# First edge pass of a graph network: target numbers spread over the partitions by TensorE instead of by a broadcast DMA

## The reference, cut to what matters

```
ef = concat([x[src], x[dst]], axis=1)        # 100000 x 256
h  = ef @ W1.T + b1
h  = relu(batchnorm(h, g1, be1))             # mean and variance over the edges
h  = h @ W2.T + b2
eu = relu(batchnorm(h, g2, be2))
x  = layernorm(x + segment_sum(eu, dst, n))
```

## Time and profile before

| | us |
|---|---|
| median of 3 runs | 4250.56 |
| lowest, highest | 4240.57, 4261.32 |
| span of the profiled execution | 4243.9 |
| first edge pass in it | 977 to 1502 |

### The profile page before, as it was taken

One profiled execution on the slowest core, in us unless ns is written; L12 is line 12 of the kernel. 1 busy time (PEld: TensorE's weight loads), 2 busy tenths in 40 slices (PEclk: granted clock), 3 DMA queues, 4 the chain that ended last, 5 costly groups with the idle time before them and its releaser, 6 DMA issues. The chain is left out here.

```text
span 4243.9 us, 85956 instructions
## 1 busy us (share of the span) xinstructions
PE 3447.9 (81%) x20439; PEld 1689.6 (40%) x20548; DVE 2654.4 (63%) x3759; ACT 1496.2 (35%) x2093; POOL 1050.2 (25%) x1132
## 2 busy tenths in 40 slices
PE   3777767686677978888898998599889989989996
PEld 1333333243344556666645554233322233332223
DVE  6877766522233455554202223699989989989995
ACT  2134555601122222222202111221088851208883
POOL 3877774665555412221000001000010000000000
PEclk8989999978898999999899999799999999999998
DMA  2255665667787866666583774511054331103333
GB/s 62 93 168 196 213 224 193 222 248 255 240 276 253 304 214 200 179 175 171 187 276 130 246 257 143 148 61 54 23 140 132 115 116 54 62 16 128 117 123 73
DMA packets 373635, 688.38 MB, mean 162 GB/s; under 512 B 136131, under 2 KB 223297, under 8 KB 372769
## 3 DMA queue, kind: packets, MB, share of 16 engines
q1 hardware_dynamic: 236400, 361.19, 26.8%
q10 hardware_dynamic: 112052, 274.54, 18.8%
q0 software_dynamic: 25088, 51.43, 4.8%
HBM read 453.91 MB, written 208.37 MB: 156 GB/s over the span
## 5 line engine op out<-in xcount | busy, mean ns | idle before, releaser
L823 POOL DMA_INDIRECT gat<-a_table,gidx x592 | 674.3, 1139 | 259.3 <-issue 142.5
L1703 DVE SCALAR_TENSOR_TENSOR pw<-ex,c_full 128x1564 f32<-128x1564 f32 x400 | 680.8, 1779 | 35.6 <-ACT ex L1231 30.9
L1231 ACT ACTIVATE ex<-psum 128x782 f32<-128x782 f32 x800 | 610.4, 826 | 77.4 <-PE psum L2114 58.9
L1665 DVE CUSTOM_DVE_ANT_0 masked<-psum,masks 128x1784 bf16<-128x1784 f32 x320 | 551.7, 1784 | 64.8 <-ACT masks L1204 43.7
L1752 PE MATMUL psum<-one_src,one_dst 128*128 x1968 | 417.7, 351 | 208.9 <-DVE one_dst L1399 127.6
L1397 DVE TENSOR_SCALAR one_src<-iota_sub,src_low 128x800 f16 x984 | 382.6, 430 | 191.7 <-PE psum L1752 124.7
L2123 PE MATMUL psum<-pw,vaug 128*32 128x391 f32 x3200 | 348.6, 508 | 30.2 <-DVE pw L1703 10.0
L1752 PEld LDWEIGHTS psum<-one_src,one_dst 128*128 x1968 | 189.4, 100 | 422.9 <-issue 340.4
L1539 DVE SCALAR_TENSOR_TENSOR u<-psum,u 128x1024 f16<-128x1024 f32 x98 | 120.0, 1225 | 254.8 <-ACT u L1109 254.8
L1204 ACT ACTIVATE masks<-masks,far 128x3128 bf16<-128x3128 bf16 x40 | 115.5, 2900 | 423.4 <-DMA masks<-ct_parts 423.4
L1067 ACT ACTIVATE r<-psum,vec 128x1024 f32<-128x1024 f32 x98 | 118.0, 1205 | 398.7 <-PE psum L1898 331.4
(11 more groups left out here) (357 smaller groups left out, 4792.0 us busy)
## 6 DMA issues: line engine op xcount, KB each, us to landing
c_full<-c_whole SPq DMA_DIRECT2D x80, 977.5 KB, 5.0
r_edges<-r ACTq DMA_DIRECT2D x98, 512.0 KB
r_in<-r_edges ACTq DMA_DIRECT2D x98, 512.0 KB, 3.7
c_ring<-ct_parts SPq DMA_DIRECT2D x100, 480.0 KB, 4.4
c_whole<-c_sum ACTq DMA_DIRECT2D x100, 400.0 KB
a_edges<-gat SPq DMA_DIRECT2D x148, 256.0 KB, 2.6
a_in<-a_edges ACTq DMA_DIRECT2D x74, 512.0 KB, 5.6
c_ring<-ct_parts SPq DMA_DIRECT2D x100, 320.0 KB, 3.6
```

Of the source, the lines that this page charges most:

```text
L823: g.indirect_dma_start(to, None, a_table, bass.IndirectOffsetOnAxis(ap=gidx[:, s, k:k + 1], axis=0)).then_inc(landed, 16)
L1231: a.activation(ex[:, step_slot(n // 2), (n % 2) * 2 * CW:(n % 2 + 1) * 2 * CW].rearrange("p (h t) -> p h t", h=2), psum[:, o:o + 2 * BANK] ...
L1665: v.tensor_tensor_reduce(out=masked[:, n % 2, 0:count * width].rearrange("p (c t) -> p c t", c=count), in0=psum[:, first * BANK:(first + c ...
L1703: v.scalar_tensor_tensor(pw[:, step_slot(k), :].rearrange("p (h t) -> p h t", h=HQ), ex[:, step_slot(k), :].rearrange("p (h t) -> p h t", ...
```

## The change

The numbers no longer go through DRAM. `edge_half` is kept in SBUF until the pass (it moves ahead of the tiles that later stages reuse; they start behind it). For unit g, TensorE multiplies a 98 x 128 matrix, the g-th column of the identity repeated 128 times, by `edge_half`: each of the 128 output partitions then holds row g, the unit's 1024 numbers. The two matmuls write the PSUM banks that layer 1 of the same unit uses afterwards. VectorE copies them from PSUM into `dst_bc` as f16 (two buffers are left of four) and signals `dst_taken`; layer 1 waits for that in place of `r1_made`, and the spread has the wait for `r1_made`. The order in TensorE's queue becomes layer1(g), spread(g+1), layer2(g-1), layer1(g+1), spread(g+2), layer2(g), ... The DMAs, the memset, and the semaphores `dst_loaded` and `dst_used` go.

```diff
-    dst_half = nc.dram_tensor("dst_half", (WP, EP // WP), f16).ap()
-    dst_flat = dst_half.rearrange("(o a) e -> o (a e)", o=1)
+        edge_at = at[0]
+        edge_half = sb("edge_half", [WP, EP // WP], f16)
         base = at[0]
...
-        dst_bc = sb("dst_bc", [P, 4, UE], f16)
+        dst_bc = sb("dst_bc", [P, 2, UE], f16)
...
-            sp.dma_start(dst_half, edge_half[:, :]).then_inc(S["a_stored"], 16)
...
             def fetch(j, q, s):
                 i = 2 * j + q
-                after(act, S["h1_psum"], 2 * i + (s - 3))
                 if not (q and s):
+                    after(act, S["h1_psum"], 2 * i + (s - 3))
...
-                after(act, dst_used[s], i + -1)
-                act.dma_start(dst_bc[:, 2 * q + s, :], dst_flat[:, ds((2 * i + s) * UE, UE)].broadcast_to([P, UE])
-                              ).then_inc(dst_loaded[2 * q + s], 16)
...
-                    hold("dve", dve, dst_loaded[2 * q + s], 16 * j + 16)
+                    dve.wait_ge(S["dst_spread"], g + 1)
+                    v.tensor_copy(dst_bc[:, s, :], psum[:, s * UE:(s + 1) * UE]).then_inc(S["dst_taken"], 1)
+                    hold("dve", dve, S["dst_taken"], g + 1)
...
-                    after(dve, dst_used[s], i)
-                    v.memset(vec[:, 30 + s:31 + s], 0.0).then_inc(dst_used[s], 1)
...
-                after(pe, S["r1_made"], 2 * i + s - 1)
+                pe.wait_ge(S["dst_taken"], 2 * i + s + 1)
...
+            def spread_dst(i, s):
+                g = 2 * i + s
+                after(pe, S["r1_made"], g - 1)
+                for half in range(2):
+                    last = t.matmul(bank(2 * s + half), identb[0:WP, ds(g, 1)].broadcast_to([WP, P]),
+                                    edge_half[:, half * GE:(half + 1) * GE], start=True, stop=True)
+                last.then_inc(S["dst_spread"], 1)
...
+            spread_dst(0, 0)
             layer1(0, 0, 0)
+            spread_dst(0, 1)
             layer1(0, 0, 1)
+            spread_dst(1, 0)
             layer2(0, 0)
...
                         layer1(j + (1 - q), q, 0, odd)
+                        spread_dst(i, 1)
                         layer2(i + -1, 1)
                         layer1(j + (1 - q), q, 1, odd)
+                        spread_dst(i + 1, 0)
                         layer2(i, 0)
```

More of the change, by code:

```diff
@@ L230, in gnn @@
         edge_order = sb("edge_order", [WP, EP // WP], i32)
-        edge_half = sb("edge_half", [WP, EP // WP], f16)
         pair_lim = sb("pair_lim", [WP, 2, NPAIR // WP], i32)
@@ L289, in gnn @@
         below_top()
-        at[0] = base
+        at[0] = edge_at
         bv_bc = sb("bv_bc", [P, P], f32)
@@ L353, in gnn @@
                  "window_done one_ready deg_psum deg_taken visit_free visit_ready dve_features agg_ready agg_sum weff_ready "
-                 "hT_next s_free s_psum m_parts_ready attn_ready attn_psum out_psum").split()
+                 "dst_spread dst_taken hT_next s_free s_psum m_parts_ready attn_ready attn_psum out_psum").split()
         S = {n: sem(n) for n in names}
@@ L359, in gnn @@
         a_loaded = [sem(f"a_loaded{s}") for s in range(3)]
-        dst_loaded = [sem(f"dst_loaded{s}") for s in range(4)]
-        dst_used = [sem(f"dst_used{s}") for s in range(2)]
         r1_stored = [sem(f"r1_stored{s}") for s in range(2)]
@@ L599, in _ @@
                          a_parts[:, :, :, :].rearrange("p b m f -> p b (m f)")).then_inc(S["a_stored"], 16)
-            sp.wait_ge(S["a_stored"], 32)
+            sp.wait_ge(S["a_stored"], 16)
             stage_end("sp", sp, None)
@@ L1506, in pass1 @@
                         v.tensor_scalar(oht[:, ds((before + b) & 1, 1), :].rearrange("p o e -> p (o e)"),
-                                        dst_bc[:, 2 * q + s, :], nodec[:, ds(b, 1)], None,
+                                        dst_bc[:, s, :], nodec[:, ds(b, 1)], None,
                                         ALU.is_equal).then_inc(S["visit_ready"], 1)
-                    after(dve, dst_used[s], i)
-                    v.memset(vec[:, 30 + s:31 + s], 0.0).then_inc(dst_used[s], 1)
                     if not isinstance(i, int):
```

## The result

The changed kernel takes 4222.3 us (median of 6 runs, 4207.2 to 4233.2) against 4248.3 us (median of 6, 4240.6 to 4261.3): a ratio of 0.9934, 95% interval 0.9917 to 0.9951, 28 us less (21 to 35). The profiled execution took 4225.1 us with a span of 4223.4. The forecast was 4222.6 us. That the total is met to 0.3 us is luck: the interval alone is 7 us wide to either side, and the terms of the sum were not met, as the stretches show.

What follows compares the result with a forecast made beforehand. Gathers bound the pass up to unit 67, TensorE afterwards. First stretch -12, middle -24, last +8 and the rest 0 sum to -28 us from the median of 4250.6, giving 4222.6, with ends 4207 to 4240; the wider range was 4180 to 4266.

Steps and rivals of the forecast that it cites:

- What bounds the kernel: First edge pass, 525 us: POOL's gathers set the pace up to unit 67, TensorE in the last 30 units.
- The relief for the gathers (36 us): First two stretches: removing the broadcasts takes 31% of 117 us excess, 12 us in the first and 24 in the middle.
- my upper end: Gathers' relief counted by loads alone: broadcasts are 24.5 of 61.5 MB, 40%, so 47 us of the excess.
- The first stretch (-12): Start of the pass: 12 of the 36 us of gather relief fall here.
- The stalls in the last stretch (-7): Last 30 units: 7 us of TensorE idle time, mostly short a_direct waits, should go with faster gathers.
- The time added per unit (0.5 us): TensorE: two matmuls 0.43 us, at most 0.07 for the copy behind layer 2; +15 us over the last 30 units.
- 307 of 497, no bound: VectorE in the pass: 98 copies of 1.22 us raise its busy time from 188 to 307 of 497 us.
- Gathers run free: Rival for the pass: TensorE is the bound throughout, 4.33 us a unit, -70 us, 4181; chance 0.15.
- Gathers do not notice: Rival for the pass: first 390 us unchanged, only the last 30 units pay 8 to 15 us, 4261; chance 0.18.
- The copy in series: Rival at TensorE's wait before layer 1: exposed spread and copy give 5.72 us a unit, +46, 4297; chance 0.09.
- the lock of the two-port mode: VectorE's copy locking GpSimd out of DMA descriptors: up to 120 us if it applied, nothing with an operand in PSUM.
- The 22% relief: Gathers, by DMA queue turns: relief at the all-bytes end, 24.5 of 110.5 MB, with the sum about 4233.

Runs made afterwards that it cites:

- The removal alone: Kernel before, with the broadcast issued for the first four units only and later units comparing against those numbers: ratio 0.9891, 46 us less.
- the earlier spread: Changed kernel with the spread of unit g+1 issued between row matmuls and visits of unit g: ratio 0.9931; with late groups also moved, 0.9919.
- the store: Changed kernel plus a 256 KB store from SBUF to DRAM per unit where the broadcast was issued: ratio 1.0015.
- the moved groups and the earlier spread: Changed kernel with both edits, spread issued before the visits and POOL's late groups moved: ratio 0.9919, 4208.8 us.
- the late groups moved: Changed kernel with none of POOL's late groups before the fifth direct unit: ratio 0.9910, 4206.5 us; same edit on the kernel before: 0.9984.
- a version that is another 25 us faster: Changed kernel with early spread, late groups moved, and the copy made by ScalarE ahead of its relu: ratio 0.9874, 4201.3 us.

## Why the prediction was right, step by step

- **What bounds the kernel.** Right: gathers up to unit 67, TensorE behind it. The removal alone gives 33 us in the middle stretch, and TensorE's stretch moves by what is put on TensorE.
- **The relief for the gathers (36 us).** The mechanism was right, the size too small. The removal alone took the middle stretch from 259.6 to 226.4 us with 141 pieces: the excess over 1.27 us a piece fell from 79.3 to 47.3 us, 40%, where I had 31%. That is the number of my upper end, but its reason was wrong: stores weigh as much as loads. The broadcasts are 12 MB of 54 in this stretch (with a_in and the stores of r), and a removed MB was worth 2.7 us where the average one costs 1.5. Put back into the changed kernel, the same 12 MB cost less: the excess rises from 39.5 us (145 pieces) to 56.7 with half (141) and 63.3 with all (142), 2.0 us a MB, 2.9 for the first half and 1.1 for the second. So that the excess rises faster than the load, as the group times of 5.1, 7.3 and 8.3 us suggest, is not borne out; why the removal was worth more than its share is open. In the change itself the middle stretch gave 36 us, but TensorE set the pace at its end.
- **The first stretch (-12).** It gave 8 us. The wait at unit 3 hardly shrank, from 15.1 to 14.2 us, and the one at unit 19 fell from 23 to 7 us (forecast 12), but the units ahead of it are longer by the added time.
- **The stalls in the last stretch (-7).** The removal alone shows 8.2 us.
- **The time added per unit (0.5 us).** The term that was mis-sized most: 144.8 less 121.2 us over 30 units is 0.79. The two matmuls add 0.29, less than the 0.43 I counted; the copy adds 0.49, and I had 0.07. The failing step is "one is 0.12", the price of a hand-over. From the end of the spread to the copy it is 0.46 us in the timeline above (0.24 on average), from the copy to the one-hot 0.67 each time. With 1.22 between them the first one-hot is ready 2.84 us after the spread's end, and layer 2 plus rows, 2.75 us that begin 0.16 before that end, do not cover it; a second visit has no cover. A second step failed beside it. I took VectorE's "307 of 497, no bound" and its statistics as "over by then". They are, but the copy comes at least 0.59 us behind their end, 0.9 on average, and busy time leaves out this gap and the 0.67. In the change itself the profile still puts 113.6 us of VectorE's idle time down to the spread; with the earlier spread VectorE's round is the bound.
- **Their sum.** That it came out is luck. Four errors stood against each other: gain in the middle 12 us too small, addition in the last stretch 8.6 us too small, the last stretch's relief 1.2 us too small, first stretch 4 us too large. I had counted the added time as hidden in the middle (206 us of work in 236). Units of 4.66 us, 48 of them, are 224 us: they set the pace there, about where the gathers stood anyway.
- **The rivals.** "Gathers run free" came half true: no wait of weight is left behind unit 19, which I had named as a sign against the forecast, and all a_direct waits together are 22 us, not near half of 103. But the units are 4.7 and not 4.3 us. "Gathers do not notice" is excluded by the removal alone. The copy in series came in part, 0.49 of 1.4 us, far from where it decides.
- **Beside the copy.** The pieces take 138.61 / 145 = 0.956 us beside the copies, after 0.960. So in the length of a piece the lock of the two-port mode is not seen with an operand in PSUM; this agrees with the second page of the Trainium skill that the prediction named (VectorE: DVE Perf Modes, Why PSUM operands drop a tier).
- **The turns of the DMA queues.** The Trainium skill (DMA: Bandwidth & Descriptors, Queues, rings and completion order) says that a DMA engine takes turns between the queues that have work, a packet at a time. I drew from it that the direction of the bytes does not matter, and the store agrees (247.7 and 243.6 us). The 22% relief that I also drew from it was too small: the removal gave 40%.
- **Open.** The span fell by 20.5 us where the pass fell by 29; the rest is spread over the later stages, none of whose code differs. I did not settle what varies there; it may also be what kept the moved groups and the earlier spread, 16 us better in the pass, from showing that in the time.

## What to carry to other kernels

Before moving a broadcast from DMA to TensorE and a copy, add up the copying engine's whole round, with the gaps at its own semaphores, and not its busy time. Put the copy on the engine with the most room in its round. What a DMA costs others is best measured by taking it out: here a removed MB was worth nearly twice the average one, in a stretch with a DMA share of 0.79, and no share of the bytes had said so. And when a total comes out right, check the terms stretch by stretch: here two large errors cancelled. Finding them, with the late groups moved, led to a version that is another 25 us faster.

## What the runs showed that I had not expected

- VectorE needs 0.67 us from the end of a copy to a dependent instruction that waits on its semaphore and enters a loop, in all 98 units, where two one-hots follow each other after 0.25 us.
- Two 98-row, 512-column matmuls in front of the fp32 matmuls of layer 2 take 0.43 us but lengthen a unit by only 0.35 (0.29 in the mean of the last stretch), since layer 2 takes 1.72 us behind them in place of 1.80.
- Ahead of the copy VectorE is idle 0.85 us on average in the kernel with the earlier spread, and nothing in its profile says for what.
- A 256 KB store slows gathers as much as a 256 KB broadcast load that reads the same 2 KB for all partitions: 247.7 and 243.6 us in the middle stretch.
